# Patch embedding without transpositions in a vision transformer on one NeuronCore, in one block with the normalisation

## What is computed

```python
def _patchify(x):                       # B, C, H, W, P, D = 64, 3, 224, 224, 16, 192
    x = x.reshape(b, C, hp, P, wp, P)   # hp = wp = 14
    x = x.transpose(0, 2, 4, 1, 3, 5)
    return x.reshape(b, hp * wp, C * P * P)
tokens = jnp.einsum('bnf,fd->bnd', _patchify(x), W) + b
seq = jnp.concatenate([cls, tokens], axis=1) + pos_table[None, :, :]
h = h + attention(layernorm(h), ...)    # its inputs and weights are rounded to 8-bit integers
h = h + mixture_of_experts(layernorm(h), ...)
```

## Time and profile before

| | us |
|---|---|
| median of 3 runs (lowest, highest) | 2128.96 (2125.84, 2130.21) |
| the profiled execution | 2127.63 |
| its span, first to last instruction | 2125.9 |
| PE busy | 1531.2 (72%) |
| DVE busy | 1486.6 (70%) |
| ACT busy | 1361.7 (64%) |
| POOL busy | 1176.2 (55%) |
| embedding: first data used, last product's row added | 41.1 to 330.9 |
| first normalising ACTIVATE | 363.9 |

### The profile page before, as it was taken

How to read it: one execution, slowest core, us unless ns; L and a number is a source line. 1 busy time by engine, 2 the same in 40 slices (tenths; PEclk the granted TensorE clock), 3 DMA queues, 4 the chain that set the end, 5 groups by cost and what they waited for, 6 DMA issues and landing times. The chain is left out here.

```text
span 2125.9 us, 51836 instructions
## 1 busy us (share of the span) xinstructions
PE 1531.2 (72%) x12472; PEld 1032.7 (49%) x12473; DVE 1486.6 (70%) x3745; ACT 1361.7 (64%) x3884; POOL 1176.2 (55%) x1918
## 2 busy tenths in 40 slices
PE   1999993785656656555378886888864999993654
PEld 1999992441111111111244443554434988883553
DVE  0555556897777777777556666788876777765996
ACT  0222221543999999999689995777762766663553
POOL 2333330005666666666155554477775888875886
PEclk9999996896555555555555555555556999996776
DMA  5444320001222122122344443544433555553774
GB/s 170 163 163 180 161 89 35 1 0 48 72 85 80 70 83 82 70 80 85 71 130 151 143 144 118 168 152 149 159 121 115 141 138 142 146 164 115 231 230 135
DMA packets 183979, 254.09 MB, mean 120 GB/s; under 512 B 28154, under 2 KB 147243, under 8 KB 180208
## 3 DMA queue, kind: packets, MB, share of 16 engines
q1 hardware_dynamic: 136256, 192.53, 29.3%
q0 software_dynamic: 19840, 39.17, 5.2%
q10 hardware_dynamic: 27808, 21.50, 3.2%
HBM read 140.66 MB, written 107.86 MB: 117 GB/s over the span
## 5 line engine op out<-in xcount | busy, mean ns | idle before, releaser
L984 ACT ACTIVATE exps_summed<-s,neg_shift 128x197 f32<-128x197 f32 x1184 | 482.7, 479 | 34.2 <-POOL neg_shift L851 32.9
L1021 DVE TENSOR_REDUCE score_max<-s 128x788 f32 (+2 forms) x320 | 284.7, 894 | 108.0 <-PE s L925 96.1
L984 ACT ACTIVATION_READ_ACCUMULATOR exps_summed<-s,neg_shift (+1 forms) x1184 | 304.7, 260 | 0.0
L1383 ACT ACTIVATE exps<-st,scalars 128x788 f32<-128x788 f32 (+1 forms) x320 | 246.4, 892 | 16.8 <-PE st L1292 16.8
L2063 POOL DMA_INDIRECT expert_sums<-y_tile,row_places x216 | 216.2, 1001 | 59.5 <-issue 30.3
L380 PE MATMUL mm<-w_tok,x_transposed 128*112 128x192 f32 x1344 | 238.7, 328 | 0.0
L324 ACT COPY x_transposed<-tp 128x672 f32<-128x672 f32 x112 | 80.5, 719 | 238.4 <-PE tp L371 238.4
L357 POOL TENSOR_SCALAR x_patches<-x_tile 112x768 f32<-112x768 f32 x112 | 93.1, 831 | 220.9 <-PE tp L371 181.7
L380 PEld LDWEIGHTS mm<-w_tok,x_transposed 128*112 128x112 f32 x1344 | 214.5, 178 | 0.1
L925 PE MATMUL s<-k_int,qk_int 16*128 16x197 bf16 x768 | 98.7, 355 | 139.0 <-ACT exps_summed L984 126.7
L1203 POOL TENSOR_SCALAR probs<-exps 128x788 bf16<-128x788 f32 (+1 forms) x160 | 130.0, 819 | 102.3 <-ACT exps L1383 102.0
(11 more groups left out here) (416 smaller groups left out, 4569.1 us busy)
## 6 DMA issues: line engine op xcount, KB each, us to landing
x_tile<-in_x SPq DMA_DIRECT2D x24, 1568.0 KB
z_tile<-listed_rows SPq DMA_DIRECT2D x108, 196.0 KB
v_ints<-v_slots SPq DMA_DIRECT2D x32, 480.0 KB, 2.5
v_slots_in<-v_ints SPq DMA_DIRECT2D x32, 480.0 KB, 3.6
q_ints<-qk_int SPq DMA_DIRECT2D x32, 295.5 KB, 2.5
k_ints<-k_int SPq DMA_DIRECT2D x32, 295.5 KB, 2.4
q_shifted<-q_ints SPq DMA_DIRECT2D x32, 295.5 KB, 3.6
k_ones<-k_ints SPq DMA_DIRECT2D x32, 295.5 KB, 4.4
```

The lines of the kernel that those rows point to most:

```text
L984: act.activation(gone[:, v % 2, k], ps[v % 3][:, k, 0:SEQ], ACT.Exp, scale=alpha, bias=nb[:, s, to:to + 1], accum_out=p.lsum[:, bass.ds(n ...
L1021: dve.tensor_reduce(columns(m, u), src, op=ALU.max, axis=AXL.X).then_inc(max_done, 1)
L1383: act.activation(ex[:, v % 4, 0:size(u)], src, ACT.Exp, scale=alpha, bias=p.col(C_LNSA)).then_inc(e_ready, 1)
```

## The change

- No transpositions and no `x_tile` of patches. A picture's rows are the contraction: w_tok's 768 input features are taken as 48 (channel, row in patch) times 16 columns in patch, and for each of the 16 columns one product has the 48 rows on the partitions. The stationary operand is 98 patches (a half picture, `HALF`), every 32nd column of the picture row; the moving one `w_tok[:, w, :]`, 192 wide.
- Two picture rows are one piece of a transfer (`k=2`, 448 values, 1792 bytes), so a load brings them to 8 partitions a channel, 24 a picture. ACT copies the even rows to partitions 64a to 64a + 23 of `xc`, POOL the odd ones to 64a + 32 to 64a + 55; rows between hold zeros in data and weights. a = 0, 1 are two pictures n and n + 32, a pair; there are 32 pairs, two slots.
- Per pair PE does two halves h of 16 columns x 2 pictures = 32 products (each two instructions in fp32) into `mm[h]`, picture a in bank a. DVE adds and takes the statistics for both pictures at once, 98 partitions.
- Stores are one a picture, 98 partitions of 384 values.
- Embedding and normalisation are one block: attention weights are loaded by ACT at the start, their maxima and integers are made by DVE within and behind the last pair, turned in fp32 ahead of the maxima's exchange; bias parts, the ones in `xq_t` and `w_slots` go to POOL. The loop takes one picture a turn, 64 turns of 2 x 98 rows instead of 56 of 2 x 112.
- The rows stand in order now, so L1402 and L1403 become one operation of 197 columns.

The diff, cut:

```diff
+    HALVES = PATCH // 2
+    ROWS2 = C_IMG * HALVES
+    def load(sp, i, s, a):
+        for ch in range(C_IMG):
+            rows = I["x"][bass.ds(SLOTS * i + s + a * PAIRED, 1), ch].rearrange("o (hp r k) w -> (o r) hp (k w)", r=HALVES, k=2)
+            at = 64 * a + HALVES * ch
+            sp.dma_start(xs[at:at + HALVES, s, :].rearrange("p (hp x) -> p hp x", x=2 * HW), rows).then_inc(x_in[2 * s + a], 16)
+    def half_rows(eng, sem, wait, i, s, k):
+        n = SLOTS * i + s
+        for a in range(2):
+            if a == 0:
+                wait(eng, mm_done, 2 * (n - SLOTS) + 2)
+            wait(eng, x_in[2 * s + a], 48 * i + 48)
+            to = xc[64 * a + 32 * k:64 * a + 32 * k + ROWS2, s, :].rearrange("p (hp w) -> p hp w", w=HW)
+            of = xs[64 * a:64 * a + ROWS2, s, :].rearrange("p (hp k w) -> p hp k w", k=2, w=HW)[:, :, k, :]
+            if k:
+                eng.tensor_scalar(to, of, 1.0, 0.0, ALU.mult, ALU.add).then_inc(sem, 1)
+            else:
+                eng.copy(to, of).then_inc(sem, 1)
...
+    def tensor(pe):
...
+                pe.wait_ge(even, 2 * n + 2)
+                pe.wait_ge(odd, 2 * n + 2)
+                for h in range(2):
+                    t = 2 * n + h
                     need(pe, h_ready, t - 1)
-                    for k in range(KCH):
-                        last = nc.tensor.matmul(mm[w % 2][0:ROWS, 0:D], xt[:, w % 2, k * ROWS:(k + 1) * ROWS],
-                                                w_tok[:, k, :], start=(k == 0), stop=(k == KCH - 1))
-                    last.then_inc(mm_done, 1)
+                    for w in range(PATCH):
+                        for a in range(2):
+                            lo = 64 * a
+                            first = PATCH * h + w
+                            last_ins = nc.tensor.matmul(mm[h][0:HALF, a, 0:D],
+                                                        xc[lo:lo + 32 + ROWS2, s, first:first + 2 * (HALF - 1) * PATCH + 1:2 * PATCH],
+                                                        w_tok[lo:lo + 32 + ROWS2, w, :], start=(w == 0), stop=(w == PATCH - 1))
+                    last_ins.then_inc(mm_done, 1)
...
+    def vector(dve):
+        for s in range(SLOTS):
+            for a in range(2):
+                dve.memset(xc[64 * a:64 * a + 32, s], 0.0).then_inc(zeros_v, 1)
...
-                link(dve.memset(x1[D1:KB], 1.0))
...
-                        dve.tensor_scalar(o[:, bass.ds(first, 1)], src[:, 0:1], less, None, ALU.subtract)
-                        dve.tensor_scalar(o[:, bass.ds(first + 1, SEQ - 1)].rearrange("p (hp wp) -> p hp wp", wp=SIDE),
-                                          src[:, 1:SEQ].rearrange("p (wp hp) -> p hp wp", hp=SIDE), less, None,
-                                          ALU.subtract).then_inc(o_out, 1)
+                        dve.tensor_scalar(o[:, bass.ds(first, SEQ)], src[:, 0:SEQ], less, None, ALU.subtract).then_inc(o_out, 1)
```

More of the change, by code:

```diff
@@ L38 @@
 PB = 8
-ROWS = PB * SIDE
 NG = B // PB
-KCH = C_IMG * PATCH * PATCH // 128
+HALF = (SEQ - 1) // 2
+SLOTS = 2
 EXP, HID, GATE = 8, 256, 96
@@ new lines, in embed @@
+    w_tok = p.sb("w_tok", [128, PATCH, D], F32, c)
+    posb = p.sb("posb", [HALF, 2, D], F32, c)
+    bias = p.sb("tok_bias", [HALF, D], F32, c)
+    st6 = p.sb("bn6", [HALF, 2, 2, 6], F32, c)
+    mv = p.sb("mean_var", [HALF, 2, 2, 2], F32, c)
+    crow = p.sb("class_row2", [128, D], F32, c)
+    xc = p.sb("x_halves", [128, SLOTS, HW * SIDE], F32, c)
+    xs = p.sb("x_rows", [128, SLOTS, 2 * HW * SIDE], F32, c)
+    mm = [p.ps(f"mm{k}", [128, 2, 512], F32, c) for k in range(2)]
+    bank = p.ps("weight_maxima", [128, 512], F32, c)
@@ new lines, in embed @@
+    (w_in, pos_in, id_s, pos_s, mm_done, h_ready, st_done, ag_done, mv_done, even, odd, zeros, zeros_v, h_out, cls_out, cls_st, w_max, tick_v, tick_p) = p.sems(
+        p.early, "a", "w_in pos_in id_s pos_s mm_done h_ready st_done ag_done mv_done even odd zeros zeros_v h_out cls_out cls_st w_max tick_v tick_p")
+    x_in = p.sems(p.early, "a", " ".join(f"x_in{k}" for k in range(2 * SLOTS)))
+    p.id_s, p.mm_done, p.ag_done, p.pos_s = id_s, mm_done, ag_done, pos_s
+    PAIRED = B // 2
+    ROUNDS = PAIRED // SLOTS
@@ new lines, in sync, with body @@
+    def sync(sp):
+        for s in range(SLOTS):
+            for a in range(2):
+                load(sp, 0, s, a)
+        def body(i, last):
+            for s in range(SLOTS):
+                n = SLOTS * i + s
+                for a in range(2):
+                    if not last:
+                        sp.wait_ge(even, 2 * n + a + 1)
+                        sp.wait_ge(odd, 2 * n + a + 1)
+                        load(sp, i + 1, s, a)
+                sp.wait_ge(h_ready, 2 * n + 2)
+                for a in range(2):
+                    sp.dma_start(p.hD[bass.ds(n + a * PAIRED, 1), 1:, :].rearrange("o (p h) d -> p (o h) d", p=HALF),
+                                 p.h[:, bass.ds(2 * (n + a * PAIRED), 2), :]).then_inc(h_out, 16)
+        repeat(sp, ROUNDS, body)
+        sp.wait_ge(h_out, 16 * B)
@@ new lines, in gpsimd, with body @@
+    def gpsimd(pool):
+        for a in range(2):
+            pool.memset(w_tok[64 * a:64 * a + 32], 0.0).then_inc(zeros, 1)
+            pool.wait_ge(zeros, a + 1)
+        pool.memset(p.idf[:], 0.0).then_inc(id_s, 1)
+        pool.wait_ge(id_s, 1)
+        pool.affine_select(out=p.idf[:], in_=p.idf[:], compare_op=ALU.not_equal, fill=1.0, base=0,
+                           pattern=[[-1, 128]], channel_multiplier=1).then_inc(id_s, 1)
+        pool.wait_ge(id_s, 2)
+        pool.tensor_copy(p.idb[:], p.idf[:]).then_inc(id_s, 1)
+        pool.memset(p.ones3[:], 1.0).then_inc(id_s, 1)
+        pool.iota(p.base[:], pattern=[[REGION, EXP]], base=0, channel_multiplier=0,
+                  allow_small_or_imprecise_dtypes=True).then_inc(id_s, 1)
+        pool.wait_ge(id_s, 5)
+        pool.wait_ge(zeros_v, 2 * SLOTS)
+        def body(i, last):
+            for s in range(SLOTS):
+                half_rows(pool, odd, lambda e, sem, v: need_apart(e, sem, v, tick_p), i, s, 1)
+        repeat(pool, ROUNDS, body)
```

825 lines of the change are left out of this document (399 added, 426 removed).

## The result

The changed kernel takes 2253.3 us, median of four runs (2213.2 to 2279.1), where the kernel before takes 2129.6 beside it: **1.047 of it, 95% interval 1.037 to 1.057, slower**. The ratio leaves out executions over 1.5% above the fastest of their kernel; the medians by themselves make 1.058. Forecast were 2280 us and slower. The four runs of the one kernel differ by 3%, those of the other by 0.3%; that is part of the result. The profiled execution is the fastest of the four: 2213.2 us, span 2211.4, which is 85.5 over the span before.

A forecast was written before the change was run, and what follows sets the result against it. TensorE bounds the first stage now, ScalarE attention; afterwards loads decide. 2127.6 + 158 (first ACTIVATE later) - 9 + 3 (normalisation) - 2 (attention outputs) = 2278, forecast 2280 us, range 2110 to 2570.

The forecast's parts named there:

- the loads decide: First stage: loads of x to 8 partitions each take 476 us, 15 a pair; last piece lands at 495 us.
- The row of 81 GB/s: Profile row of L761's 16-partition copies, taken as the nearest rate for the new 8-partition loads of x.
- the prediction's paragraph on ports: Loads of x: four neighbouring partitions share a port, so 8 make two, 54 GB/s; about 2510 us in all.
- the signs to look for: First stage if right: 10.4 us product bursts after 4 to 5 us waits, pairs every 15, first ACTIVATE about 522.
- the first rival: First stage: loads keep up above 145 GB/s, TensorE never short, first ACTIVATE at 365.6, 2121 us in all; chance 0.20.
- the products: TensorE, first stage: 4096 halves at 0.163 us, two at a time, 334 us, 10.4 a pair; 51 us more than before.
- The third rival: TensorE takes 668 us: products not overlapping, weight loads up to twice 0.082 us, or half clock; 2455 in all; chance 0.15.
- the price of weight loads: TensorE's products: 0.082 us per load of 98 columns, from L1679; four per pair of products are 0.33 us against 0.326.
- the start: Before the first product: with loads keeping up, products begin at about 18 us, after four MEMSETs (10.5 us) and two copies.
- costs nothing: SyncE's queue: waiting for `h_ready` of pair n between the loads of n + 2 and n + 3 adds no time.
- the end: From the last loaded piece to the first normalising ACTIVATE: copy, products, VectorE's rows, weight integers and chain, 27 us, so 522.
- Normalisation and attention: After the first ACTIVATE: weight work -9 us, 128 normalising operations at 345 ns +3, attention outputs -2.

The follow-up runs named there:

- 3: Changed kernel with every second of the 16 patch columns left out of the products, loads, copies and stores kept: 2391.3 us, 12.7 us a pair.
- 5: Changed kernel with each load's 8 rows per channel on every third partition instead of 8 neighbours: ratio 1.0174 to the kernel before.
- 6: Changed kernel with rows on every third partition and half of the products left out: 2102.4 us, 9.0 us a pair.
- 4: Changed kernel with all loads behind the second pair left out, later pairs using the same rows: 2338.7 us, 46 over the kernel before.
- 9: Changed kernel with rows on every third partition and 98 neighbouring columns as stationary operand, so other columns multiplied: 2146.9 us.
- 8: Changed kernel with rows on every third partition, class-row store and attention-weight loads moved later on ScalarE's queue: 2149.4 us, 1.0097.
- 7: Changed kernel with SyncE storing pair n - 1 behind the loads of n + 2: 2214.1 us, 1.0413.
- 1: Changed kernel run again unaltered, on a chip where the kernel before takes 2293 us: 2406.5 us, 1.036.
- 2: Changed kernel run once more unaltered, on a chip where the kernel before takes 2287 us: 2411.6 us, 1.057.

## Why the prediction was right, and where it was off

**Right: the loads decide.** "This is the term that decides", and the partitions that a load fills are why: runs 3, 5 and 6 show it, with 12.7 us a pair for the loads alone and 9.0 once the partitions are spread. The term was over-sized: a pair took 12.3 to 13.4 us, not 15, all of x came at 84 to 90 GB/s up to the last piece, where the forecast's 495 us make 78, and the last copy began at 427 to 459, not 495.

**Luck: how near the price came.** The row of 81 GB/s does not say what was read from it. The prediction sets it beside 220 and 349 GB/s "at the same engine load", but its DMA share is 0.40 where theirs are 1.08 and 1.04: in that 0.47 us the engines stood idle for more than half of the time, with one small transfer. It shows no price of 16 partitions in a stream of loads, let alone of 8. That 81 lay near the rate measured, and 2280 within 27 us of a median whose executions spread over 66 us, is in part luck. That the partitions are the mechanism is not, since run 5 changes them alone. But it is not their number, as the sum had it: run 5's loads still fill 8 partitions each, only further apart, which is what the prediction's paragraph on ports makes of it.

**Off: the signs to look for.** I named bursts of 10.4 us with 4 to 5 us before them, a pair every 15. With 12.3 against 10.9 what is left are 18 gaps; the profile alone would have passed for the first rival. Only taking TensorE's work away (3) and the loads away (4) tells them apart.

**Off: the products.** 0.163 us a half, two at a time, 334 us: two at a time they are (the third rival's main half is out), but every 171 ns for two makes 350. The step that failed is the price of weight loads, 0.082 us from L1679's neighbouring columns: loads of every 32nd column cost 5% (9). The third rival's half on them was that mechanism at a twentieth of its price.

**Off: the start.** The first rival let the products begin at 18 us. They begin at 47.5. At 239 ns a packet only 0.50 MB of the first pair's 1.2 had come by 10 us, from then to 30 us the tables on ScalarE's queue took 55% of the engines' time, and the second picture came at 32.6 (by 17.4 with the rows spread). And ScalarE stood until 40.35 behind its own wait for the class row's sum, which waited for tables that came at 38.9. I had priced the MEMSETs and the copies and not what stands ahead of the copies on ScalarE's queue. In the sum this hid under the loads, which are issued from 0.8 us on; in the rival it did not.

**So the first rival's time was false even with no loads behind the second pair.** It put the ACTIVATE at 365.6; `no_reload` has it at 413.9, 48 later, 29.5 by the start and 18 by the products (352 for 334). With the start mended too (8) the new embedding is still 21 us over the kernel before.

**SyncE's order "costs nothing".** In doubt: 229 us of waiting became 78 and the last product came 12 us or more earlier (7), but the gain is not told apart from the spread of the changed kernel.

**Right: the end.** 14 us from the last product (441.4) to the ACTIVATE and 28.5 from the last copy's data, for 27 forecast.

**Normalisation and attention.** First ACTIVATE to first row written into `xq_t`: 4.0 us for 12.4, -8.4 (forecast -9). The 128 operations of L697 last 369 ns on average, for 345 forecast, and the stretch grows by 5 us (forecast +3). The merged L1402 gave nothing measurable: from `attend`'s first exponential to its last output operation are 264.7 us for 265.0 (forecast -2). From the first ACTIVATE to the end 1756.2 for 1762.0 us.

**The sum** with what was measured in the profiled execution: +91 at the first ACTIVATE (forecast +158), -6 behind it (forecast -8), +85.5 in all (forecast +150). At the median it is +124, on the other two chips +114 and +124, since the profiled execution was the one with the least gaps. Nearly all that is missing is the loads' term.

## What to carry to other kernels

An engine that is 96% busy isn't thereby the bound: look whether what feeds it ever waits for anything but its own source, and take half of the engine's work away. The rate of the loads here went by the partitions that each reaches, and to spread the same rows over three times as many neighbours was a change of one index in the load, with the weights' rows in the same order. And a layout that saves transpositions can lose more in the array: 96 of 128 rows, 98 of 128 columns and strided weight loads make 10.9 us for 392 patches, 27.9 ns each, where 2.53 us for 112 were 22.6 with the transpositions in it and 16.9 without. Of the factor 1.65 between 27.9 and 16.9, (128 x 112) / (96 x 98) = 1.52 is the part of the array that is used; the rest is the 171 ns for two halves where 158 stood.

## What the runs showed that I had not expected

Some of VectorE's operations last until a copy of GpSimd's ends. In the run with spread rows the position table's sum, 0.56 us elsewhere, took 2.87 and ended just behind GpSimd's copy:

```profile
27.49 2.80 POOL L305 TENSOR_SCALAR x_halves<-x_rows 24x3136 f32<-24x3136 f32 x1 [7.34 <-DMA x_rows<-in_x]
27.82 2.87 DVE L415 TENSOR_TENSOR posb<-posb,tok_bias 98x384 f32<-98x384 f32 x1 [12.93 <-DMA class_row<-in_L_tok_pos_table]
```

In the changed kernel the same befalls the four-column copy of L470, which takes 0.17 us when GpSimd is idle:

```profile
151.44 2.80 POOL L305 TENSOR_SCALAR x_halves<-x_rows 24x3136 f32<-24x3136 f32 x1 [2.18 <-DMA x_rows<-in_x]
151.74 2.54 DVE L470 COPY h_mean_var<-mean_var 98x4 f32 x1
...
443.72 0.17 DVE L470 COPY h_mean_var<-mean_var 98x4 f32<-98x4 f32 x1
```

27 of its 64 copies are drawn out so, 47 us together, and the bn_stats and reductions beside them are not. The Trainium skill, SBUF — State Buffer, section "Who interferes with whom", calls it an exclusive lock of a port pair that VectorE and GpSimd share. It costs nothing here, since VectorE waits for products 145 of the 340 us from 100 to 440, but it would if VectorE were the bound.

Copies on ScalarE and on GpSimd that step by 32 or 98 fp32 elements take twice the time of those that run through (5.7 to 6.1 for 2.80 us), on both engines alike. The Trainium skill, SBUF — State Buffer, section "Door 1: The DMA port swizzle", says that each access that goes on to a new 16-byte line pays for it, which agrees with that and with the weight loads' 254 for 162 ns; no run here varied the step to show where it sets in, and copies that move the columns in twos or fours were not tried. And the DMA engines' busy share is no measure of their rate: 0.57 with 130 GB/s and with 168. It stays at 0.56 or 0.57 in every window from 100 to 300 us in which the loads set the pace (1, 2, 3, 6), nine engines' worth with the stores in it. Whether loads of more than 8 rows would keep more engines at work was not tried.
